# Last layer of a four-layer kernel: two image rows of a sample turned together and summed by the tap matmul

## The reference

```python
x_off = g_lt[:, None] * gather(q_lt_x, q_lt_y) + g_rb[:, None] * gather(q_rb_x, q_rb_y) \
      + g_lb[:, None] * gather(q_lt_x, q_rb_y) + g_rt[:, None] * gather(q_rb_x, q_lt_y)
mm = (m * ad_m).transpose(0, 2, 3, 1)[:, None]
x_off = x_off * mm
x_off = x_off.reshape(b, c, h, w, ks, ks).transpose(0, 1, 2, 4, 3, 5)
x_off = x_off.reshape(b, c, h * ks, w * ks)
return conv2d(x_off, w_conv, None, ks, 0)
```

## Time and profile before

| What | us |
|---|---|
| Plain runs, median of 3 | 12763.94 |
| Plain runs, lowest and highest | 12756.97 and 12778.16 |
| Profiled execution: span from the first to the last instruction | 13258.5 |
| POOL busy in the span | 7518.9 |
| PE busy | 7451.2 |
| DVE busy | 6180.1 |
| ACT busy | 4757.6 |

### The profile page before, as it was taken

The page is one execution under the profiler, slowest core; times in us unless marked ns, Lnnn a source line. Parts: engine busy times, 40 slices in busy tenths (PEclk is TensorE's granted clock), DMA queues, the critical chain, the costliest instruction groups (busy, mean ns, idle before and its releaser), DMA issues. The chain is left out here.

```text
span 13258.5 us, 114790 instructions
## 1 busy us (share of the span) xinstructions
PE 7451.2 (56%) x29878; PEld 2708.4 (20%) x29878; DVE 6180.1 (47%) x8631; ACT 4757.6 (36%) x7391; POOL 7518.9 (57%) x7857
## 2 busy tenths in 40 slices
PE   7786776778777676853289992333232323233332
PEld 2222222222222222221123321111111111111111
DVE  1344444444433444445456664454455445545444
ACT  7664554646555454641156661111111111111100
POOL 0375655657565564757500004777777767767776
PEclk9897887889888787876599995565565656555665
DMA  0232232223322222337633337343434343433332
GB/s 9 66 96 87 85 93 80 87 89 96 92 85 79 89 85 86 91 94 172 164 86 81 82 78 139 101 121 101 120 97 119 101 111 98 120 97 101 100 96 90
DMA packets 1169072, 1280.23 MB, mean 97 GB/s; under 512 B 795966, under 2 KB 924414, under 8 KB 1164670
## 3 DMA queue, kind: packets, MB, share of 16 engines
q0 software_dynamic: 338688, 925.30, 23.5%
q1 hardware_dynamic: 815710, 347.84, 11.1%
q10 hardware_dynamic: 14368, 3.21, 0.1%
HBM read 1080.00 MB, written 195.82 MB: 96 GB/s over the span
## 5 line engine op out<-in xcount | busy, mean ns | idle before, releaser
L423 POOL DMA_INDIRECT b_gathered<-table,b_iu x3528 | 3701.6, 1049 | 1929.9 <-issue 1013.0
L423 POOL DMA_INDIRECT d_gathered<-table,d_iu x3528 | 3705.2, 1050 | 1420.4 <-issue 1041.0
L526 PE MATMUL PS<-ident,d_sample 128*128 128x128 f32 (+1 forms) x1960 | 509.6, 424 | 2978.1 <-DVE d_sample L879 2090.9
L504 PE MATMUL PS<-b_key 64*128 64x448 f32 (+1 forms) x5600 | 1516.6, 622 | 448.9 <-ACT b_weights L665 300.1
L665 ACT ACTIVATE b_weights<-PS 128x896 f32<-128x896 f32 (+1 forms) x1400 | 1270.1, 907 | 1287.5 <-remote 882.8
L861 DVE TENSOR_TENSOR d_gathered<-d_gathered,PS 128x2304 f32<-128x2304 f32 x392 | 1000.9, 2553 | 1184.1 <-DMA d_gathered<-table,d_iu 1115.1
L514 PE MATMUL PS<-b_weights,b_values 128*64 128x448 f32 (+1 forms) x5600 | 1462.9, 603 | 123.1 <-issue 73.4
L668 ACT ACTIVATE b_weights<-b_weights 128x896 f32<-128x896 f32 (+1 forms) x1400 | 1332.3, 952 | 44.7
L674 ACT ACTIVATE d_sampleT<-PS 128x512 f32<-128x512 f32 x392 | 233.6, 596 | 2894.4 <-PE PS L526 2000.9
L526 PEld LDWEIGHTS PS<-ident,d_sample 128*128 128x128 f32 (+1 forms) x1960 | 336.0, 205 | 3130.8 <-issue 2721.1
L866 DVE TENSOR_TENSOR b_gathered<-b_gathered,PS 128x1152 f32<-128x1152 f32 x392 | 529.9, 1352 | 819.3 <-DMA b_gathered<-table,b_iu 802.6
(11 more groups left out here) (227 smaller groups left out, 9679.5 us busy)
## 6 DMA issues: line engine op xcount, KB each, us to landing
b_gathered<-table,b_iu POOLq DMA_INDIRECT x3528
d_gathered<-table,d_iu POOLq DMA_INDIRECT x3528
l_x_and_h<-xs SPq DMA_DIRECT2D x224, 224.0 KB, 3.9
hs<-l_hT SPq DMA_DIRECT2D x224, 224.0 KB, 2.8
d_h<-hs SPq DMA_DIRECT2D x32, 1554.0 KB
table<-b_table_rows SPq DMA_DIRECT2D x208, 128.0 KB, 2.0
table<-d_table_rows SPq DMA_DIRECT2D x208, 128.0 KB
xs<-b_key SPq DMA_DIRECT2D x14, 1568.0 KB
```

The costliest lines, as they stand in the source:

```text
L423: pool.indirect_dma_start(GB[:, g, k, :], None, tables[b], bass.IndirectOffsetOnAxis(ap=ix, axis=0)).then_inc(gathered[g], 16)
L504: mm = pe.matmul(PS[0:keys(k), 2 * (k % S_BUFS) + a, 0:CH], KEY[r, 0, k * P:k * P + keys(k)], KEY[r, 0, j * CH:(j + 1) * CH], start=True, ...
L526: mm = pe.transpose(PS[0:n, 5 + 2 * (s // 4), (s % 4) * P:(s % 4 + 1) * P], S[:, t % 2, s * P:s * P + n], K.ident[:, :])
```

## The change

In the last layer DVE no longer adds the two rows. A tap's 128 columns, 64 of the top row and 64 of the bottom row, stay side by side in the gathered buffer, and PE turns all 128 at once: 9 turns of 128 columns per tile, straight from the gathered buffer, into PSUM banks 2, 3 and 4. ACT copies 8 of them in one instruction and the ninth in another. `ST` and the weights `WK` have 9 slabs in place of 5. The weights of each tap stand twice in WK, on partitions 0 to 63 and 64 to 127, so that the tap's matmul, which sums over partitions, adds the rows. `apply_taps` has 18 matmuls in place of 10. The buffer of gathered rows is now freed by PE's turns (samplesT_mm) instead of by DVE, and S is gone. In b_ nothing changes.

```diff
-        ST = sb("sampleT", [P, 5, 2 * CH])
+        SLABS = 5 if att else TAPS
+        ST = sb("sampleT", [P, SLABS, 2 * CH])
...
-        WK = sb("wk", [P, 5, C])
-        S = sb("sample", [P, 2, TAPS * C])
+        WK = sb("wk", [P, SLABS, C])
+        S = sb("sample", [P, 2, TAPS * C]) if att else None
...
+        TURNED = 2 if att else TPC
...
+            even, odd = (taps[0::2], taps[1::2]) if att else (taps, taps)
+            sp.dma_start(WK[0:C, :, :], even.rearrange("k c o -> c k o")).then_inc(w_loaded, 16)
+            sp.dma_start(WK[C:P, 0:4 if att else TAPS, :], odd.rearrange("k c o -> c k o")).then_inc(w_loaded, 16)
...
-                        wait_apart(pool, samples_ready, c * TPC + t + 1 - BACK[t] + TPC)
+                        wait_apart(pool, samples_ready if att else samplesT_mm, c * TPC + t + 1 - BACK[t] + TPC)
...
+                if not att:
+                    for k in range(TAPS):
+                        mm = pe.transpose(PS[:, 2 + k // 4, (k % 4) * P:(k % 4 + 1) * P],
+                                          GB[:, t % G_BUFS, k, 0:P], K.ident[:, :])
+                    mm.then_inc(samplesT_mm, 1)
+                    return
...
-                    for s in range(5):
-                        n = P if s < 4 else C
+                    for s in range(SLABS):
+                        n = C if att and s == 4 else P
...
-                act.wait_ge(samplesT_mm, c * TPC + t + 3)
+                act.wait_ge(samplesT_mm, c * TPC + t + 1 + TURNED)
+                if not att:
+                    act.activation(ST[:, 0:8, t * P:(t + 1) * P],
+                                   PS[:, 2:4, :].rearrange("p n (s f) -> p (n s) f", s=4), ACT.Copy)
+                    act.activation(ST[:, 8, t * P:(t + 1) * P], PS[:, 4, 0:P], ACT.Copy).then_inc(samplesT_ready, 1)
+                    return
...
-                v.wait_ge(weighed, (c * TPC + t) * 2 + 2)
-                v.tensor_tensor(gx[:, :, 0:P], gx[:, :, 0:P], gx[:, :, P:2 * P], ALU.add).then_inc(weighed, 1)
+                v.wait_ge(weighed, (c * TPC + t) * (2 if att else 1) + 2)
+                v.tensor_tensor(gx[:, :, 0:P], gx[:, :, 0:P], gx[:, :, P:2 * P], ALU.add)\
+                    .then_inc(weighed if att else samples_ready, 1)
...
-                            else:
+                            elif att:
                                 add_rows(c, t)
```

More of the change, by code:

```diff
@@ L285, in _ @@
                     sp.dma_start(BV[a * C:(a + 1) * C, :], att[1]).then_inc(w_loaded, 16)
-            sp.dma_start(WK[0:C, :, :], taps[0::2].rearrange("k c o -> c k o")).then_inc(w_loaded, 16)
-            sp.dma_start(WK[C:P, 0:4, :], taps[1::2].rearrange("k c o -> c k o")).then_inc(w_loaded, 16)
+            even, odd = (taps[0::2], taps[1::2]) if att else (taps, taps)
+            sp.dma_start(WK[0:C, :, :], even.rearrange("k c o -> c k o")).then_inc(w_loaded, 16)
+            sp.dma_start(WK[C:P, 0:4 if att else TAPS, :], odd.rearrange("k c o -> c k o")).then_inc(w_loaded, 16)
             def load(src, i, to):
@@ L391, in _ @@
             pool.sem_inc(samples_ready, TPC)
-            pool.sem_inc(samplesT_mm, 2)
+            pool.sem_inc(samplesT_mm, TURNED)
             pool.sem_inc(samplesT_ready, 1)
@@ L533, in apply_taps @@
                 for a in (0, 1):
-                    for s in range(5):
-                        n = P if s < 4 else C
+                    for s in range(SLABS):
+                        n = C if att and s == 4 else P
                         mm = pe.matmul(PS[a * C:(a + 1) * C, 7, 0:CH], WK[0:n, s, :], ST[0:n, s, a * CH:(a + 1) * CH],
-                                       start=(s == 0), stop=(s == 4), skip_group_check=True)
+                                       start=(s == 0), stop=(s == SLABS - 1), skip_group_check=True)
                 mm.then_inc(conv_done, 1)
```

## The result

| | before | after |
|---|---|---|
| Plain runs, median | 12767.92 us (6 runs) | 12727.44 us (6 runs) |
| lowest and highest | 12753.04, 12778.16 | 12715.73, 12739.02 |
| ratio to before | | 0.9966, 95% interval 0.9956 to 0.9976 |
| span of the profiled execution | 13258.5 us; a second one 12759.4 us | 12734.2 us |

The forecast was 12855 us, slower by 0.7%. The kernel became faster by 0.34%, 40 us. The forecast was wrong in its sign, and the time lies outside its range.

A forecast was written before the change was run, and what follows sets the result against it. GpSimd's gathers were taken as the pace. Terms -22 + 15 + 55 + 9 + 7 gave +64 us, late chunks +30: +94 on the median 12763.94, rounded down to 12855 us. Its own range was 12815 to 12910, overall 12780 to 12930.

The forecast's parts named there:

- row sums' own hits: Last layer, mainly each chunk's third tile: removed row sums no longer stretch gathers; 22 us gained, 32 at most.
- later chunk heads, other phases: Usual chunks: VectorE's first tiles start 6.6 us later, column sums meet gathers at other phases; +15 us, bounds -20 to +40.
- six changes of pair: Fifth tile at each pair change: GpSimd waits for TensorE's turn of the first tile, 9.2 us each; +55 us.
- start: Layer's start: GpSimd's wait for a buffer ends later, at TensorE's turn instead of VectorE's row sum; +9 us.
- end: After the last gather: nothing hides the longer taps; +6.6 us, entered as +7.
- late chunks: Chunks where ScalarE and VectorE come 20 to 50 us late: longer buffer waits, up to 85 us, a third taken: +30.
- The release of a buffer: Last layer: GpSimd's buffer wait moves from VectorE's row sum to TensorE's turns, four tiles deep where it was six.
- A usual chunk stays within 1 us of 90.4: Sign expected in the changed profile: length of a usual seven-tile chunk nearly unchanged; longer chunks would show the forecast wrong.
- Rival 1: Last layer: late chunks are as frequent in plain runs; +149 us, 12913 us; chance 22%.
- 2 (pair change hidden): Pair changes: the later buffer release costs nothing there, only +9 us is left, 12773 us; chance 13%.
- Rival 3: Tiles 4 to 6 of late chunks: GpSimd's waits for row sums disappear; -133 us, 12631 us; chance 4%.
- Rival 4: All 392 tiles: every row sum stretches a gather through the port, so removal gives -141 us, 12623 us; chance 5%.

The follow-up runs named there:

- c0: The unchanged kernel before, profiled again as an undisturbed control; 12761.26 us in one run.
- g1: The changed kernel with an unread dummy row sum on VectorE, one of its two operands read from PSUM; 12804.35 us, ratio 1.0006.
- f1: The kernel before without the last layer's row sums and with 8 more tap matmuls per chunk into an unread PSUM bank; 12687.46 us, ratio 0.9921.
- f2: The changed kernel with only 10 of its 18 tap matmuls per chunk; 12770.65 us, ratio 0.9987.
- e3: The kernel before with 8 more tap matmuls (16 passes) per chunk into an unread PSUM bank; 12766.4 us, ratio 0.9996.
- e1: The kernel before without the last layer's row sums, its sample buffer zeroed once; 12733.94 us, ratio 0.9971.
- g0: The changed kernel, unaltered, run again on another chip; 12740.62 us, ratio 0.9955.
- g2: The changed kernel with 4 more tap matmuls (8 passes) per chunk into an unread PSUM bank; 12781.74 us, ratio 0.9989.
- e2: The changed kernel with an unread dummy row sum on VectorE, both operands in SBUF; 12806.28 us, ratio 1.0026.
- f3: The changed kernel with five buffers of gathered rows in the last layer in place of four; 12678.21 us, ratio 0.9913.

## Why the prediction was wrong

The layer took 43.0 us less than in c0 (5103.4 to 5060.4). Its sum by the prediction's own terms:

| term | forecast | measured |
|---|---|---|
| row sums' own hits | -22 | -30 |
| later chunk heads, other phases | +15 | -69 |
| six changes of pair | +55 | +41 |
| start | +9 | +6 |
| end | +7 | +4 |
| late chunks | +30 | 0 |
| sum | +94 | -48 |

**The step that failed** is the one on collisions: "The one that mattered little now costs like a random one ... 49 x 0.3 = +15 us", with its bounds of -20 to +40. The true value is outside them. A usual chunk became 2.02 us shorter, 97 us in 48. Adding up the excess of the gathers under column sums, c0 has 5.12 us a chunk and after 3.69: 1.43 x 48 = 69 us; the rest is the row sums' 30. By the tile whose column sum stretched the gather, the hits moved like this (us per chunk, mean of the 48):

| tile | 1 | 2 | 3 | 4 | 5 | 6 | 7 |
|---|---|---|---|---|---|---|---|
| c0 | 0.34 | 0.74 | 0.96 | 0.50 | 0.87 | 0.87 | 0.84 |
| after | 0.49 | 0.11 | 0.17 | 0.33 | 0.87 | 0.90 | 0.84 |
| g1, dummy | 0.44 | 0.76 | 0.64 | 0.42 | 0.86 | 0.90 | 0.84 |

Only the first tile got dearer, as the step said; the second and third lost most of it, and with the dummy sum (g1) they have it back. The step looked at that one sum and called its new phase random, at random's price. But VectorE does the first four tiles as one chain behind the taps, each sum's place set by the lengths ahead of it, and two of those lengths changed at once (0.76 us less per tile, taps and eviction later). All four sums were moved, and the bounds had been taken for one. In c0 the four cost 2.53 us a chunk; at 0.1 us each they would cost 0.4, at 0.97 us each 3.9. So the bounds for 49 chunks were about -100 to +70, wide enough to leave the sign of the whole open. f1 and f2 show that the shift of the chain does it and that both edits are needed; g1 shows that even an instruction that stretches no gather costs 64 us through it.

Why both are needed can be read from the traces for the second tile. First the sums of tiles 1 and 2 of a usual chunk in after (no row sum), then in e3 (row sum and long taps):

```profile
9424.30 1.36 DVE L886 TENSOR_TENSOR d_gathered<-d_gathered 128x1152 f32<-128x1152 f32 x1
9424.89 1.59 POOL L426 DMA_INDIRECT d_gathered<-table,d_iu  x1 [0.30 <-issue]
9426.78 0.95 POOL L426 DMA_INDIRECT d_gathered<-table,d_iu  x1 [0.30 <-issue]
9428.03 0.95 POOL L426 DMA_INDIRECT d_gathered<-table,d_iu  x1 [0.30 <-issue]
9428.16 1.36 DVE L886 TENSOR_TENSOR d_gathered<-d_gathered 128x1152 f32<-128x1152 f32 x1
9429.29 1.05 POOL L426 DMA_INDIRECT d_gathered<-table,d_iu  x1 [0.30 <-issue]
```

```profile
9153.89 1.36 DVE L875 TENSOR_TENSOR d_gathered<-d_gathered 128x1152 f32<-128x1152 f32 x1
9154.35 1.71 POOL L423 DMA_INDIRECT d_gathered<-table,d_iu  x1 [0.30 <-issue]
9156.37 0.95 POOL L423 DMA_INDIRECT d_gathered<-table,d_iu  x1 [0.30 <-issue]
9157.62 0.95 POOL L423 DMA_INDIRECT d_gathered<-table,d_iu  x1 [0.30 <-issue]
9158.63 1.36 DVE L875 TENSOR_TENSOR d_gathered<-d_gathered 128x1152 f32<-128x1152 f32 x1
9158.87 1.93 POOL L423 DMA_INDIRECT d_gathered<-table,d_iu  x1 [0.30 <-issue]
```

A stretched gather ends 0.82 us after the sum that stretched it, and the next ones start 0.30 and 1.55 us later: a hit sets the gathers' places anew, at 1.12 and 2.37 us after the sum's end. If VectorE then goes straight on, its next column sum starts 2.50 us after the last one's end, 0.13 us behind a gather's start, and costs little; with a row sum between them it starts some 3.4 us after, a quarter of a microsecond ahead of a gather, and costs nearly a whole one. It goes straight on only when it is late. In the second tile it first had to wait for the gathers in 42 of the 48 usual chunks of c0, 47 of e1 and all 48 of f2, and the sum then cost 0.72 to 0.87 us. With long taps (e3, f1, after, g0, g1, g2, e2) it waited in none: the sum costs 0.92 us with the row sum (e3), 0.77 and 0.76 with a dummy (e2, g1), and 0.18, 0.11, 0.11 and 0.10 without one (f1, after, g0, g2). So the long taps take the wait away, and the missing row sum puts the sum where it hits little. In the third tile VectorE waited in 46, 45 and 48 chunks of c0, e1 and f2 and in one of each of the runs with long taps. The second tile's place could thus have been worked out beforehand; for the first, third and fourth, which lie behind other work, it was not tried.

**The late chunks** (+30) are the second miss. The text saw that 494 us were missing from the plain runs and put a third of the term into the sum. c0 has none of these waits. Without this term the forecast would have been 12828, still wrong in sign.

**What held.** The release of a buffer did move from VectorE's sum to TensorE's turn; the fifth tile of each chunk at a change of pair waits, 9.5 to 11.7 us of idle GpSimd, 0.9 of it usual, where 9.2 was forecast. The price is a little smaller, +6.8 us a chunk, since the same chunk gained elsewhere. f3 takes the wait away, and the gain is what it cost. The usual chunk waits for no turn, its margin 12.3 us at the least and 13.3 at the median (forecast 14). The eviction takes 1.02 us (forecast 0.6 + 0.4). The taps take 14.6 us (median; c0 10.7) where 16.6 was forecast: about 4 more instead of 6.1, which also explains start and end. The 0.38 us from pass to pass came as forecast, but where the second image's passes follow the first's, four of the 36 start 0.06 us or less after the one before. "A usual chunk stays within 1 us of 90.4" failed, on the good side: 87.3, where c0 has 89.35.

**The rivals.** Rival 1 (late chunks frequent) and 2 (pair change hidden) are refuted. Rival 3, faster since waits for the row sum vanish, was right in sign and wrong in cause: c0 has 6.1 us of such waits. Rival 4, every row sum stretches a gather, is the nearest in kind; but it bets on 227 us of the row sums themselves, and they had 30. The Trainium skill ("SBUF — State Buffer", section "SBUF: two separate sides") has a two-input VectorE op hold the shared port for the whole instruction, the loser blocking fully. c0 and after agree, for a gather that starts while the op is running; they show as well that a gather that starts 0.12 us before the op takes its usual 0.94 and the op its usual 1.36, so that there neither blocks, against the rule. What the rule does not give, and what made this result, is which of the two comes first.

## What to carry to other kernels

Where one engine is the pace and another can stretch its instructions, do not count the hits that an edit removes: lay the whole chain of the other engine against the pace at its new times, for each of the steps between two resynchronisations, before you give that term a sign. Here two lengths were enough for one step: where a hit leaves the engine that sets the pace (its next gather starts 0.82 + 0.30 us after the sum's end), and when the other engine starts its next sum (2.50 us after it). If it can't be laid out, take the bounds from all the ops that move. And rather than look for a good phase, take away the op that can hit at all: moving the column sums too to TensorE, which had room, took 172 us off the version with five buffers.

## What the runs showed that I had not expected

- In the traces a gather (0.95 us) that starts while a sum of two SBUF operands is running ends 0.82 us after that sum, whatever the sum's length: column sum 9429.15 + 1.36 = 9430.51, gather's end 9431.33; dummy sum 8103.02 + 0.76 = 8103.78, gather's end 8104.60; column sum 9442.78, gather's end 9443.59. So it loses time only if it starts more than about 0.13 us before the sum's end. Of the gathers of c0 that start so under a column or row sum, 432 of 444 end 0.82 us after it; the other 12 start within 0.04 us of the sum's start, and take 0.94 or 0.95 us. The normalization of the next pair, which has no second tensor among its operands, stretches gathers too (c0: it ends at 8346.63, a gather of 2.23 us at 8347.45).
- Leaving work out can cost time: 8 tap matmuls fewer per chunk made the changed kernel slower, from 0.9966 to 0.9987 of before.
- One profiled execution lay 499 us above a second one of the same kernel (13258.5 and 12759.4), 410 of them before the last layer began.
- In c0 a row sum that starts 0.04 us before a gather does not stretch it (0.94 us) and itself takes 0.83 instead of 0.76 us: the loser can be VectorE.

```profile
9432.83 0.83 DVE L879 TENSOR_TENSOR d_sample<-d_gathered 128x576 f32<-128x576 f32 x1 [0.21 <-DVE d_lo L802]
9432.87 0.94 POOL L423 DMA_INDIRECT d_gathered<-table,d_iu  x1 [0.30 <-issue]
```
